# Retention loop: scaling and casts moved from VectorE to ScalarE, with the decay mask as an operation of its own

## What is computed

```python
qkv = x @ W_qkv                                   # x is normalised
q, k, v = split(qkv); split_heads                 # 16 heads, 64 wide, T = 2048
ret   = einsum('bhtd,bhsd->bhts', q, k) * decay   # decay = gamma_h ** (t - s) for t >= s, else 0
inner = einsum('bhts,bhsd->bhtd', ret, v)
cross = einsum('bhtd,hde->bhte', q, past_kv) * 1024
r = inner + cross                                 # then a norm over all of r, and x + r
```

## Time and profile before

| | |
|---|---|
| median of 2 runs | 7430.58 us (7407.33 to 7453.83) |
| the profiled execution | 7426.18 us, span 7424.5 us on its slowest core |
| spans of the 8 cores | 7382.4 to 7424.5 us |
| mean granted clock of TensorE | 0.682 to 0.688 of full speed |
| busy: TensorE, VectorE, ScalarE | 54%, 42%, 16% of the span |
| stages of one batch | load 86 us, norm 110, retention 991, norm 139, gates 204, feed-forward 2120, store 146 (first batch, with what lies between; the borders are rounded) |

### The profile page before, as it was taken

One profiled execution on the slowest core, in us unless ns is written; L12 is line 12 of the kernel. 1 busy time (PEld: TensorE's weight loads), 2 busy tenths in 40 slices (PEclk: granted clock), 3 DMA queues, 4 the chain that ended last, 5 costly groups with the idle time before them and its releaser, 6 DMA issues.

```text
span 7424.5 us, 71604 instructions; the slowest of 8 cores (7382.4 to 7424.5 us)
## 1 busy us (share of the span) xinstructions
PE 3975.6 (54%) x18802; PEld 1976.2 (27%) x18936; DVE 3081.2 (42%) x11415; ACT 1193.9 (16%) x2157; POOL 86.2 (1%) x102
## 2 busy tenths in 40 slices
PE   4555554344664665574455454543446655745655
PEld 1222222222322322232222222322223222322322
DVE  4444444554334333423444444445543334234334
ACT  2000002121311221222020000021213212211220
POOL 0000000000000000000000000000000000000000
PEclk9756565567776786786656565655667867867866
DMA  2100000000000000000011000000000000000001
GB/s 56 18 5 9 5 1 0 13 8 11 8 8 8 11 4 8 11 4 1 33 59 18 5 9 5 1 0 13 8 11 8 7 8 11 4 8 11 4 1 46
DMA packets 114453, 84.81 MB, mean 11 GB/s; under 512 B 55663, under 2 KB 105202, under 8 KB 114066
## 3 DMA queue, kind: packets, MB, share of 16 engines
q0 software_dynamic: 101536, 45.49, 5.1%
q1 hardware_dynamic: 12530, 34.75, 1.3%
HBM read 108.93 MB, written 16.78 MB: 17 GB/s over the span
## 4 chain that ended last, share of the span: by engine, by line
PE 46%; DVE 30%; issue 14%; ACT 7%; DVEq 1%; DMA 1%; another core or an unknown queue 0%; ACTq 0%; POOL 0%; SPq 0%; POOLq 0%
PE PA L983 13%; ACT ETb L1105 5%; PE PA L1215 4%; DVE gac L1020 3%; DVE ztk L1179 3%; PE PBF L1193 3%; PE PA L1114 3%; DVE stc L633 2%; DVE zp L1198 2%; PE PB L556 2%; DVE xT L1222 2%; PE PA L534 2%; PE PA L640 2%; PE PB L1099 2%; PE PB L628 2%
## 5 line engine op out<-in xcount | busy, mean ns | idle before, releaser
L983 PE MATMUL PA<-wb,xnT 128*128 128x320 bf16 x6144 | 999.7, 332 | 215.3 <-ACT q5t L989 212.0
L1105 ACT ACTIVATE ETb<-PB,smc 128x512 bf16<-128x512 f32 x1024 | 657.7, 685 | 1283.8 <-PE PB L1099 817.8
L983 PEld LDWEIGHTS PA<-wb,xnT 128*128 128x128 bf16 x6144 | 655.1, 108 | 542.3 <-issue 222.9
L1193 PE MATMUL PBF<-identb,ztk 128*128 128x128 bf16 (+1 forms) x768 | 203.2, 265 | 817.7 <-DVE ztk L1179 570.4
L989 ACT CAST q5t<-PA 128x320 bf16<-128x320 f32 x768 | 325.9, 425 | 1883.2 <-PE PA L983 1538.1
L1114 PE MATMUL PA<-ETb,vag 128*128 128x512 bf16 x1000 | 397.4, 397 | 197.8 <-ACT ETb L1105 190.6
L1215 PE MATMUL PA<-zp,wo_hat 128*128 128x512 bf16 x1248 | 343.0, 426 | 230.4 <-DVE xT L1222 221.8
L1020 DVE SCALAR_TENSOR_TENSOR gac<-q5t,ggt,gac 128x64 f32<-128x64 bf16 x2304 | 455.1, 277 | 0.0
L1099 PE MATMUL PB<-qfT,kfT 128*128 128x512 bf16 x986 | 398.2, 408 | 28.6 <-ACT ETb L1105 15.7
L1136 DVE CAST oTb<-PA 65x1024 bf16<-65x1024 f32 x32 | 39.1, 1221 | 795.2 <-PE PA L1114 795.2
L1198 DVE COPY zp<-PBF 128x128 bf16<-128x128 bf16 (+1 forms) x768 | 172.0, 224 | 401.1 <-PE PBF L1193 401.1
(11 more groups left out here) (229 smaller groups left out, 4942.7 us busy)
## 6 DMA issues: line engine op xcount, KB each, us to landing
wb<-Wkv POOLq DMA_DIRECT2D x32, 640.0 KB, 7.0
xs<-x SPq DMA_DIRECT2D x32, 512.0 KB
y<-ys SPq DMA_DIRECT2D x32, 512.0 KB
wb<-Wq POOLq DMA_DIRECT2D x16, 640.0 KB, 6.9
wqt<-Wqkv POOLq DMA_DIRECT2D x16, 256.0 KB, 4.5
wkt<-Wqkv POOLq DMA_DIRECT2D x16, 256.0 KB, 5.9
wvt<-Wqkv POOLq DMA_DIRECT2D x16, 256.0 KB, 6.5
wo_hat<-Wo_hat POOLq DMA_DIRECT2D x1, 1280.0 KB, 17.1
```

What stands on the lines that cost most here:

```text
L983: mmq = pr.emit("tensor", (lambda aa, tt, bk, pa2: lambda te: te.matmul(PA[:, bk * 512:bk * 512 + 320], xnT[:, aa * T + tt * 128:aa * T + ...
L1105: ex_prev[j] = pr.emit("scalar", (lambda jj, s2, p2, p_: lambda sc: sc.activation(out=ET[:, s2 * 512:(s2 + 1) * 512], in_=PB[:, p2 * 512:( ...
L1193: tpz = pbf_wr(bank2, (lambda tt, l2, w2, rb2, bk: lambda te: te.transpose(PBF[rb2:rb2 + w2, bk * 1024 + 256:bk * 1024 + 256 + 128], z_tok ...
```

## The change

Three things in `emit_retention`, all of them numerically the same up to the rounding of an intermediate:

1. L589 and L594, the scaling of the transposed K chunks, go from VectorE (`tensor_scalar`) to ScalarE (`activation` with Identity and the column as scale).
2. L609 and L666, the casts of the state to bf16, go from VectorE to ScalarE (`copy`).
3. L633 is split in two: ScalarE scales the scores from PSUM into `st_ch` (bf16), and VectorE then multiplies `st_ch` by the mask, in place, from SBUF. The second waits for the first, and all that waited for L633 waits for the second.

```diff
-                e1 = pr.emit("vector", (lambda cc2, bk, pp: lambda v: v.tensor_scalar(
+                e1 = pr.emit("scalar", (lambda cc2, bk, pp: lambda sc: sc.activation(
                     out=ktokS[:, cc2 * 128:cc2 * 128 + 64],
-                    in0=PBF[:, bk * 1024:bk * 1024 + 64],
-                    scalar1=gkcols[:, (2 * pp) * 16 + cc2:(2 * pp) * 16 + cc2 + 1],
-                    scalar2=None, op0=OP.mult))(c, bank, p), waits=[ktr])
+                    in_=PBF[:, bk * 1024:bk * 1024 + 64], func=AF.Identity,
+                    scale=gkcols[:, (2 * pp) * 16 + cc2:(2 * pp) * 16 + cc2 + 1]))(
+                        c, bank, p), waits=[ktr])
...
-                mcast0 = pr.emit("vector", (lambda bs: lambda v: v.tensor_copy(
+                mcast0 = pr.emit("scalar", (lambda bs: lambda sc: sc.copy(
                     out=Mbf[bs:bs + 64, :], in_=Msb[bs:bs + 64, :]))(base), waits=[mz])
...
-                    ev = pr.emit("vector", (lambda cc2, hq, bk, sl: lambda v: v.scalar_tensor_tensor(
+                    sc_ev = pr.emit("scalar", (lambda cc2, hq, bk, sl: lambda sc: sc.activation(
                         out=st_ch[:, sl * 128:(sl + 1) * 128],
-                        in0=PB[:, bk * 512:bk * 512 + 128],
-                        scalar=gkcols[:, hq * 16 + cc2:hq * 16 + cc2 + 1],
-                        in1=dmasks[:, 0:128],
-                        op0=OP.mult, op1=OP.mult))(c, h, bank, (2 * c + hh) % 4),
+                        in_=PB[:, bk * 512:bk * 512 + 128], func=AF.Identity,
+                        scale=gkcols[:, hq * 16 + cc2:hq * 16 + cc2 + 1]))(
+                            c, h, bank, (2 * c + hh) % 4),
                         waits=[mmst, sv_last])
+                    ev = pr.emit("vector", (lambda sl: lambda v: v.tensor_tensor(
+                        out=st_ch[:, sl * 128:(sl + 1) * 128],
+                        in0=st_ch[:, sl * 128:(sl + 1) * 128],
+                        in1=dmasks[:, 0:128], op=OP.mult))((2 * c + hh) % 4),
+                        waits=[sc_ev])
...
-                        mcast = pr.emit("vector", (lambda bs: lambda v: v.tensor_copy(
+                        mcast = pr.emit("scalar", (lambda bs: lambda sc: sc.copy(
                             out=Mbf[bs:bs + 64, :], in_=Msb[bs:bs + 64, :]))(base),
                             waits=[madd])
```

More of the change, by code:

```diff
@@ L588, in emit_retention @@
                     waits=[ev_kT, ktr_prev.get(c - 2)])
-                e1 = pr.emit("vector", (lambda cc2, bk, pp: lambda v: v.tensor_scalar(
+                e1 = pr.emit("scalar", (lambda cc2, bk, pp: lambda sc: sc.activation(
                     out=ktokS[:, cc2 * 128:cc2 * 128 + 64],
-                    in0=PBF[:, bk * 1024:bk * 1024 + 64],
-                    scalar1=gkcols[:, (2 * pp) * 16 + cc2:(2 * pp) * 16 + cc2 + 1],
-                    scalar2=None, op0=OP.mult))(c, bank, p), waits=[ktr])
-                e2 = pr.emit("vector", (lambda cc2, bk, pp: lambda v: v.tensor_scalar(
+                    in_=PBF[:, bk * 1024:bk * 1024 + 64], func=AF.Identity,
+                    scale=gkcols[:, (2 * pp) * 16 + cc2:(2 * pp) * 16 + cc2 + 1]))(
+                        c, bank, p), waits=[ktr])
+                e2 = pr.emit("scalar", (lambda cc2, bk, pp: lambda sc: sc.activation(
                     out=ktokS[:, cc2 * 128 + 64:(cc2 + 1) * 128],
-                    in0=PBF[:, bk * 1024 + 64:bk * 1024 + 128],
-                    scalar1=gkcols[:, (2 * pp + 1) * 16 + cc2:(2 * pp + 1) * 16 + cc2 + 1],
-                    scalar2=None, op0=OP.mult))(c, bank, p), waits=[ktr])
+                    in_=PBF[:, bk * 1024 + 64:bk * 1024 + 128], func=AF.Identity,
+                    scale=gkcols[:, (2 * pp + 1) * 16 + cc2:(2 * pp + 1) * 16 + cc2 + 1]))(
+                        c, bank, p), waits=[ktr])
                 ktr_prev[c] = e2
```

## The result

The changed kernel takes 7560.2 us (median of 12 runs, 7536 to 7617) against 7428.2 us (10 runs, 7398 to 7460). The ratio, from which the one slow run of the changed kernel (7617 us, with half of the chip at a lower granted clock) is left out, is 1.0172, with a 95% interval of 1.0145 to 1.0200: 128 us slower (108 to 149), where 186 us were forecast with a range that began at 7572 us. So the kernel became slower for the reason that was given, but by about 60 us less, and within 2%.

The account below looks back on a forecast made before the run. The retention stage was taken as a chain of short steps with no engine full; 176 us (score step) plus 10 us (K transposes) made 186 us, so 7617 us, 2.5% slower, range 7572 to 7690 us.

Parts of the forecast that it names:

- Step 1: Score step L633 split over ScalarE and VectorE: 0.344 us more on the chain, 512 times, 176 us.
- Step 2: State's bf16 copy (L666, L609) to ScalarE: costs nothing, 1.1 us of cover; its removal from VectorE gains nothing.
- Step 3: Scaled K transposes (L589, L594) on ScalarE: 0.97 us against 0.88 for two chunks, 112 rounds, 10 us.
- Step 4: ScalarE table loads: no new one counted; one at each of four stage changes would be 5 us.
- A: Score step: mask product runs at one element per cycle, 0.068 us more per chunk, 35 us, 7652 us; chance 0.17.
- C: ScalarE's queue: state copy unfinished when the scaling behind it is ready; 26 us more, 7643 us; chance 0.09.
- D: Retention chunk: VectorE's own queue is the bound, so 0.44 us a chunk goes away, 7205 us; chance 0.03.
- B: ScalarE scalings: the scale costs no pointer time, 0.092 us less per chunk, 7550 us; chance 0.14.

Follow-up runs that it names:

- the swap: Kernel before with only L662's two waits reordered, the state's cast named ahead of the product L655: 7364.6 us, ratio 0.9921.

## Why the prediction was wrong, step by step

- **What bounds the stage** was right: a chain of short steps, on which the score step lies and the cast and VectorE's load don't. Moving the casts alone gave 2.135 us against 2.137.
- **Step 1, the split**, was right in mechanism and nearly in size. 0.344 us were forecast; alone it cost 0.331. Its terms measured 0.368 (forecast 0.365), 0.10 (0.10) and 0.225 (0.23); the last hundredths lie in the hand-over from TensorE to ScalarE, 0.36 instead of 0.37. 512 x 0.331 = 169 us against 176.
- **Step 2, the casts: this is the step that failed.** It said that on VectorE nothing late was queued behind L666 and that its removal gains nothing. That holds for the work, not for the waits. Where the cast runs decides which counter L662 has to wait for, and with the split in place that wait is covered by another and dropped: 480 x 0.07 = 34 us back. It needs both parts, as the two runs with one part each show. The other new wait, of TensorE for the cast, cost nothing that can be seen (0.46 us from L640 to L655 in both). The rows held the sign of it: in the earlier trace rows L662 starts 0.17 us after the modelled end of L655 (247.81 + 0.26), while L633 starts 0.11 us after that of L628 (246.48 + 0.26). I took the first gap as a fixed price and never asked why it was 0.06 us longer.
- **Step 3, the K transposes**, was right: 10 us forecast, (7.67 - 7.06) x 16 = 9.8 measured.
- **Step 4**: right. The trace of the changed kernel has one table load, as before. The work between the two retention passes took 2563 us (2568 before) and that behind the second 2505 (2500), medians over the cores.
- **The sum**: 126 us in the gaps within heads, 0.32 us at each of 32 heads' last chunks (from L628 to L672, 10 us), 9.8 us in the transposes, and about 5 us given back in the q projection (below) make 141 us. The two retention passes of the trace, median over the cores, grew from 1017.8 and 1021.2 us (from the start of the first norm's last L450 to the start of the second norm's L374) to 1092.3 and 1087.4: 141 us. The runs say 128 (108 to 149), so the two agree within the interval. Of the 45 us between the forecast's 186 and these 141, the dropped wait is 34, the split 7 and the q projection 5. The dropped wait alone would have brought the forecast from 7617 to 7583 us; what is left to the measured 7560 is the other two and the spread of the runs.
- **The range** went wrong at its low end. It took in the smaller costs of the terms that I had, and no term for waits that appear or vanish. Such a term (0.07 us for each wait instruction on the chain, 34 us each way) would have put its low end at 7538 and the measured time inside.
- **The rivals**: A, C and D didn't occur. For C, the cast ended at 249.60 + 0.24 = 249.84 and the next scaling started 0.36 us after 249.66, at 250.02: 0.18 us to spare, 0.17 forecast. B's time, 7550 us, was near the measured one by accident.

## What to carry to other kernels

Where an engine isn't full and the stage is a chain, as here, moving work to an idle engine adds hand-overs to the chain and gains nothing by the relief: 0.10 us for the hand-over and 0.23 us for the second instruction, 512 times. Count the wait instructions of each step on the chain before and after a change, including those that vanish because another wait now covers them, and name the wait that is satisfied last, last: the swap alone gave 0.8% here, of which the chunks account for 0.5%. In this kernel the long step of the recurrence was better issued a turn ahead (4.9%, the swap included) than split over engines (1.7% slower).

## What was not expected of the hardware

A wait that is already satisfied costs about 0.07 us of VectorE's chain when it stands behind the late one (0.02 us of its own and 0.05 until the next), and nothing that can be seen when it stands ahead of it.

The length of the q projection after a recurrence varies from kernel to kernel although nothing in it was changed. From the last copy of `gqB` to the eviction of q it takes 9.79 us before, 9.46 in the changed kernel and 9.02 with the swapped waits (means over pairs and cores). The mean duration of L534 shows it in the groups of TensorE, of before, after and the swap:

```profile
L534 PE MATMUL PA<-xnT,wqt 128*128 128x512 bf16 x496 | 147.9, 470 | 7.9 <-issue 4.7 <-DMA wqt<-Wqkv 3.1
```

```profile
L534 PE MATMUL PA<-xnT,wqt 128*128 128x512 bf16 x512 | 149.3, 463 | 3.1 <-DMA wqt<-Wqkv 3.1
```

```profile
L534 PE MATMUL PA<-xnT,wqt 128*128 128x512 bf16 x512 | 143.9, 450 | 2.0 <-DMA wqt<-Wqkv 2.0
```

The granted clock is 0.50 all through a recurrence (1.2 GHz). In the kernel before it is still 0.50 from 324 to 328 us, where the second pair's q projection begins, and 1.00 (2.4 GHz) from 330 us on. In this projection the first eleven L534 take 631 ns each and start 0.43 us apart; the last take 379 ns and start 0.22 us apart. So a pair's first products run at the lower level until the clock rises, and how many do differs: of the 512 L534, 191 take over 500 ns before, 163 in the changed kernel and 134 with the swap (means over the cores; on two of them 16 records are missing). Over 16 pairs the projection is 5 us shorter in the changed kernel and 12 us with the swap. With the 35 us of the chunks that makes up the 48 us that the swap's retention passes gained; the 11 us from there to the 59 us of the runs lie within their interval. I have no run that shows what sets the moment at which the clock rises.
